# The last routed group takes six tiles instead of four, two tiles stay dense instead of four, and the layer norms of the last batches are moved between the gathers

## The chip, the cores and the metric

One core of one Trainium2 chip runs the whole program. The metric is device time in microseconds (us), median over runs. TensorE (PE) does the matrix products, VectorE (DVE) and ScalarE (ACT) the elementwise work, GpSimd (POOL) some elementwise work and all indirect DMAs (scatters and gathers of rows by an index), SyncE (SP) issues nearly all other DMAs.

## The reference, cut to what matters

The input is x of shape (4, 1024, 256) in float32: B = 4 batches of S = 1024 tokens. Two blocks follow each other, each added to its input and then layer-normalised (mean and variance over the 256 features, eps 1e-5, no scale or shift).

```python
x = layernorm(x + attention(x))   # 16 heads of 16, causal, window of 64 tokens back
x = layernorm(x + moe(x))

def moe(x):                                   # 4096 tokens, 256 features
    scores = sigmoid(x @ router_w.T)          # 16 experts
    sc = scores + e_bias
    # 4 groups of 4 experts; the sum of a group's two best picks 2 groups; then the 4 best experts of these
    tw = scores[chosen] / sum * 2.5           # weights of the 4 chosen experts
    y_e = (silu(x @ gate_e.T) * (x @ up_e.T)) @ down_e.T      # 128 hidden features for each of 16 experts
    return sum_over_chosen(tw * y_e) + shared(x)              # shared: the same form with 2 * 128 hidden features
```

## The kernel before, in words

A tile is 128 tokens, a chunk is 512 tokens (four tiles), a batch is two chunks, so there are eight chunks, 0 to 7. Attention runs as 16 rounds of 13 steps. Two slots belong to each step: slots are numbered h, and the attention ends at slot `tail` = 416. All mixture-of-experts work is cut into jobs, and the function `plan()` puts each job of each engine in a slot; PE takes at most one job in a slot. Every engine then walks through its own slots in order (`fill(h)`), so the plan sets the order of each engine's queue and nothing else: each job waits on semaphores for what it needs, and all behind it on that engine wait too. Slots have no fixed duration.

Every product with weights is done in three fp16 products (high by high, high by low, low by high), over two halves of the 256 features, so each output of the first layer takes six matmuls.

*Routed groups.* `GROUPS` holds four groups: three of a whole batch (eight tiles) and one of chunk 6 alone (four tiles). For a group, `chain` normalises a chunk after attention and computes the router's logits (job `lg`, L767), `route` (L1460) selects experts on DVE in parts, `pos` counts on PE, `place` (L1524) computes on DVE where each token's row goes, and POOL scatters the rows of each tile four times (L1190, one indirect DMA for each tile and choice) into a DRAM buffer `rows`, sorted by expert in units of 128 rows. A group with n tiles has 4n + 16 units, which are taken in pairs. For each pair SP loads the rows transposed (L1027), PE computes gate and up (job `gu`, L844: 24 matmuls 128 wide, whose weight address comes from a register that holds the expert), ACT and DVE apply silu and split the product (L1353, L1637, L1360, L1651), PE computes down (job `y`, L857: 12 matmuls 256 wide), ACT scales it (L1368), SP stores it to the DRAM buffer `outs` (L1033). The shared expert of two tiles is two `gu` jobs of 12 matmuls 256 wide and one `ysh` job (L869). When all pairs of a group are stored, POOL gathers four rows for each token (L1198, four indirect DMAs for each tile, into one of two buffers `yg`), DVE adds them with their weights (`combine`, L1716), and each finished chunk is normalised: moments on DVE (L1723, L1729), the power on POOL (`rstd2`, L1150 to L1156), scaling on ACT (`norm2`, L1324), store by SP (L1054).

*The dense chunk.* Chunk 7 (`DENSE`) is not routed. All 18 experts (two shared, 16 routed) run over its four tiles: job `up` (L798, 12 matmuls 512 wide), then ACT (L1341, L1347) and DVE (L1669 times the weight of the expert for each token, which SP broadcasts from `c_dram`, L1044; L1673; L1658), then job `down` (L814, 12 matmuls 256 wide) into two banks that sum over experts. `finish` (L1675) adds the sum, takes the moments, and `norm_half` and `store_half` end the program.

*What sets the order in the tail.* Behind `tail` the plan has, in this order of slots: chain and routing of chunk 6 (lg at tail+5, pos at tail+12), chain of chunk 7 (lg at tail+20), its expert weights, group 3's scatters (tail+16 to tail+26, at 1.5 to a slot), group 2's pairs until tail+45, group 3's shared and routed jobs (tail+41 to tail+90), with `up` 0 to 5 and `down` 0 to 2 between them, group 2's gathers from tail+51, group 3's gathers from tail+96, and `up` 6 to 17 and `down` 3 to 17 until tail+117.

## Time and profile before

| | us |
|---|---|
| median of 3 runs | 1179.46 |
| lowest, highest | 1176.62, 1181.22 |
| the profiled execution's own time | 1183.34 |
| its span, first to last instruction | 1181.6 |
| PE, DVE, ACT, POOL busy | 1025.7, 826.1, 624.5, 462.2 |

The profile comes from one execution with the hardware profiler on. Busy time leaves out register, branch, semaphore and DMA-issuing instructions. "Idle before, releaser" is the time that an engine sat idle ahead of an instruction, and what ended it; "issue" means that the engine waited for nothing that the profile shows. The end of a matmul is modelled, and matmuls overlap, so the pace of PE is read from start to start. PEclk is the clock granted to TensorE as a share of 2.4 GHz.

### The profile page before, as it was taken

How to read it: one execution, taken by the hardware profiler on the slowest of the kernel's cores; microseconds unless marked ns; L12 is line 12 of the kernel's file. 1: busy time of each engine (PE TensorE's matmuls, PEld its weight loads, DVE VectorE, ACT ScalarE, POOL GpSimd, SP SyncE). 2: the span in 40 equal slices, each digit the busy share in tenths (PEclk: the TensorE clock that was granted, in tenths of full speed). 3: DMA queues.
4: the chain of work that ended last, by engine and by line, in shares of the span. 5: the costliest groups of instructions: out<-in, count | busy, mean ns of one | idle time of the engine just before them, and what ended most of it. 6: DMA issues, size and time to landing. Idle time of an engine off the chain costs nothing.

```text
span 1181.6 us, 24711 instructions
## 1 busy us (share of the span) xinstructions
PE 1025.7 (87%) x8538; PEld 585.9 (50%) x8538; DVE 826.1 (70%) x1828; ACT 624.5 (53%) x1416; POOL 462.2 (39%) x676
## 2 busy tenths in 40 slices
PE   8999999898787999988968889979888864997995
PEld 4554444345332555554634445545544453775653
DVE  8788889778965676787647777687564573445575
ACT  4337777665455666654544656644464742433432
POOL 8752122332165122203627463204626735035351
PEclk9999999999888999998989989998989977998998
DMA  5772557433122454433618554523617554688451
GB/s 191 238 247 66 175 190 231 125 95 77 45 86 76 104 105 103 120 61 68 172 62 156 122 130 119 134 46 78 179 68 148 148 117 134 140 178 190 152 180 49
DMA packets 216678, 150.73 MB, mean 128 GB/s; under 512 B 134624, under 2 KB 192736, under 8 KB 216560
## 3 DMA queue, kind: packets, MB, share of 16 engines
q1 hardware_dynamic: 203184, 116.50, 39.0%
q0 software_dynamic: 10752, 29.37, 7.7%
q10 hardware_dynamic: 2624, 3.28, 0.9%
q8 instruction: 75, 1.23, 0.4%
q14 instruction: 43, 0.35, 0.1%
HBM read 52.46 MB, written 70.29 MB: 104 GB/s over the span
## 4 chain that ended last, share of the span: by engine, by line
PE 55%; DVE 19%; issue 10%; ACT 5%; POOL 4%; DMA 3%; another core or an unknown queue 2%; SPq 1%; DVEq 0%; POOLq 0%; ACTq 0%
PE bank L844 14%; PE bank L662 11%; PE bank L632 9%; PE bank L645 8%; DVE a_mx L1407 6%; PE bank L857 4%; DVE e_R L1716 2%; PE bank L635 2%; ACT a_PT L1259 2%; DMA k_dram<-p_qk 2%; PE bank L748 1%; PE bank L869 1%; PE bank L677 1%; POOL p_qk L1120 1%
## 5 line engine op out<-in xcount | busy, mean ns | idle before, releaser
L1407 DVE TENSOR_REDUCE a_mx<-bank 128x1 f32<-128x512 f32 (+3 forms) x720 | 421.1, 619 | 189.8 <-PE bank L635 95.1
L1259 ACT ACTIVATE a_PT<-bank 128x512 f32<-128x512 f32 (+4 forms) x832 | 373.2, 498 | 182.0 <-PE bank L645 151.2
L645 PE MATMUL bank<-a_QS,a_KS 113*128 113x512 f16 (+4 forms) x832 | 275.6, 339 | 23.2 <-DVE a_mx L1407 17.0
L632 PE MATMUL bank<-a_KS,a_QS 112*128 112x512 f16 (+4 forms) x832 | 264.5, 338 | 30.4 <-ACT a_PT L1259 16.5
L1145 POOL TENSOR_SCALAR_AFFINE_SELECT a_PT<-a_PT 128x256 f32<-128x256 f32 (+1 forms) x288 | 111.2, 393 | 368.6 <-ACT a_PT L1259 366.6
L662 PE MATMUL bank<-a_PT,a_VG 128*17 128x512 f32 (+4 forms) x1664 | 187.1, 518 | 4.2 <-POOL a_PT L1145 2.4
L1198 POOL DMA_INDIRECT a_pool<-outs,e_slot x112 | 111.2, 993 | 118.9 <-DMA outs<-e_ys 50.9
L1190 POOL DMA_INDIRECT rows<-e_XR,e_slot x112 | 111.8, 998 | 108.3 <-DVEq L1559 80.2
L1353 ACT ACTIVATE e_tq<-bank 128x256 f32<-128x256 f32 x116 | 44.5, 384 | 202.3 <-PE bank L844 150.5
L632 PEld LDWEIGHTS bank<-a_KS,a_QS 112*128 112x128 f16 x832 | 80.6, 99 | 134.7 <-ACT a_PT L1259 66.1
L645 PEld LDWEIGHTS bank<-a_QS,a_KS 113*128 113x128 f16 x832 | 81.8, 100 | 102.7 <-DVE a_mx L1407 37.4
L844 PE MATMUL bank<-e_xt,a_W 128*128 128x128 f16 x1416 | 112.5, 229 | 12.2 <-DVE e_hf L1644 9.6
L635 PE MATMUL bank<-a_tri,a_idb 128*128 128x128 f16 (+1 forms) x576 | 111.8, 213 | 2.1 <-issue 2.1
L844 PEld LDWEIGHTS bank<-e_xt,a_W 128*128 x1416 | 95.1, 102 | 34.8 <-issue 23.2
L857 PE MATMUL bank<-a_W,e_hh 128*128 x352 | 67.3, 288 | 7.2 <-DVE e_R L1706 3.4
L635 PEld LDWEIGHTS bank<-a_tri,a_idb 128*128 128x128 f16 x576 | 55.7, 99 | 30.3 <-issue 3.4
L662 PEld LDWEIGHTS bank<-a_PT,a_VG 128*17 128x17 f32 x1664 | 34.4, 117 | 59.3 <-issue 49.5
L1651 DVE TENSOR_TENSOR e_hl<-e_hf,e_hh 128x256 f16<-128x256 f32 x116 | 49.9, 431 | 14.7 <-ACT e_hh L1360 12.3
L1360 ACT CAST e_hh<-e_hf 128x256 f16<-128x256 f32 x116 | 47.3, 408 | 23.1 <-DVE e_hf L1644 14.7
L1716 DVE SCALAR_TENSOR_TENSOR e_R<-a_pool,e_wk,e_R 128x256 f32<-128x256 f32 x112 | 56.7, 507 | 3.5 <-DMA a_pool<-outs,e_slot 0.5
L1368 ACT ACTIVATE e_ys<-bank 128x512 f32<-128x512 f32 x88 | 52.3, 597 | 10.8 <-PE bank L857 4.4
L1637 DVE SCALAR_TENSOR_TENSOR e_hf<-bank,e_tq 128x256 f32<-128x256 f32 x34 | 14.3, 424 | 57.5 <-ACT e_tq L1353 50.0
(184 smaller groups left out, 1371.6 us busy)
## 6 DMA issues: line engine op xcount, KB each, us to landing
outs<-e_ys SPq DMA_DIRECT2D x88, 256.0 KB
rows<-a_pool SPq DMA_DIRECT2D x48, 256.0 KB, 3.6
q_dram<-p_qk SPq DMA_DIRECT2D x16, 256.0 KB, 2.8
k_dram<-p_qk SPq DMA_DIRECT2D x16, 256.0 KB, 3.9
v_dram<-p_vs SPq DMA_DIRECT2D x8, 512.0 KB, 7.2
a_QS<-q_dram SPq DMA_DIRECT2D x64, 64.0 KB
a_KS<-k_dram SPq DMA_DIRECT2D x64, 64.0 KB
a_VG<-v_dram SPq DMA_DIRECT2D x16, 256.0 KB
```

The costliest lines, as they stand in the source:

```text
L632: mm = pe.matmul(ps[:, at:at + hi - lo], QS[p][0:MR, t // NT, h, t % NT * P:t % NT * P + P], KS[p][0:MR, piece, h % 2, 0:hi - lo], start=T ...
L635: mm = pe.matmul(ps[:, at + m0 - lo:at + hi - lo], idb[:], tri[:, m0 - P * t - WIN:m1 - P * t - WIN], start=False, stop=True)
L645: pe.matmul(ps[:, 0:(qc + 1) * CH - q0], KS[p][0:MR + 1, kt // NT, h % 2, kt % NT * P:kt % NT * P + P], QS[p][0:MR + 1, qc, h, q0 - qc * C ...
L662: mm = pe.matmul(otbank[32 * h:32 * h + HD + 1, q0 - qc * CH:CH], VG[p][:, kt, h:VW:HG], PT[(p + i) % 2][:, h, 0:(qc + 1) * CH - q0], star ...
L844: mm = pe.matmul(ps[:, up * 2 * P + at:up * 2 * P + at + v], weights(e, (2 * up + lo) * D + k * P, P), tall[k][part], start=(i == 0), stop ...
L857: mm = pe.matmul(ps[:, v * D:v * D + D], o[q % NHB][:, v * P:v * P + P], weights(e, at, D), start=(i == 0), stop=(i == 2))
L1145: pool.affine_select(out=a, in_=a, compare_op=ALU.is_ge, fill=0.0, base=q0 - (kt * P - WIN), pattern=[[0, 2], [1, w]], channel_multiplier= ...
L1190: pool.indirect_dma_start(rows[b % 2], bass.IndirectOffsetOnAxis(ap=slot[b % 3][:, at, k:k + 1], axis=0), XR[:, at, :], None).then_inc(sca ...
L1198: pool.indirect_dma_start(yg[i % 2][:, k, :], None, outs[b % 2], bass.IndirectOffsetOnAxis(ap=slot[b % 3][:, at, k:k + 1], axis=0)).then_i ...
L1259: act.activation(PT[(G + i) % 2][:, h, 0:w], bank("ST", G, i, h)[:, 0:w], ACT.Exp)\
L1407: dve.tensor_reduce(mx[:, piece, t // NT, heads[0]:heads[0] + n, t % NT], bank("S", G, u)[:, 0:n * w].rearrange("p (h k) -> p h k", h=n), ...
L1716: ins = dve.scalar_tensor_tensor(zz, yg[i % 2][:, k, :], wk[b % 3][:, at, k:k + 1], zz, op0=ALU.mult, op1=ALU.add)
```

## The change

- `GROUPS`: the last group covers tiles 0 to 5 of the last batch (chunk 6 and half of chunk 7): 4 * 6 + 16 = 40 units, 20 pairs, against 32 units and 16 pairs. It needs the routing of both chunks, which is now one list `ROUTES`, and the position job `pos` of group 3 comes behind the second chunk's routing.
- The dense part keeps the last two tiles (`NDT = 2`, 256 tokens). Two experts are computed in one `up` and one `down` job: nine iterations in place of 18; each `up` has 24 matmuls 256 wide, each `down` 12 of 256, into one bank.
- The routed dense iterations (1 to 8) come no earlier than two slots ahead of the last `y` of group 3 (`AHEAD = 2`); iteration 0 (the two shared experts) may come earlier.
- Groups 2 and 3 gather into four buffers in place of two (`sum_of`, `FOUR_FROM`): two new ones lie in the attention's output `O`.
- Group 2's pairs are spread from tail-20 to tail+10 (before: tail-24 to tail).
- The last four `y` of group 3 come four slots behind their `gu` (before: seven); `store_y` comes two slots behind `y` (before: three).
- The norm of group 2's second chunk (5) and of chunk 6 come some slots later, among or behind the gathers of group 3 (`wait`). Before, chunk 6 was normalised at the very end.
- Chunk 7 ends in two halves (`end_of_halves`): tiles 2, 3 (dense) and then tiles 0, 1 (routed), each with its moments, power, shift, scaling (one tile on DVE, one on ACT) and its own store.

```diff
-GROUPS = [(b, 0, BT) for b in range(B - 1)] + [(B - 1, 0, NT)]
+NDT = 2
+DC = NDT * P
+GROUPS = [(b, 0, BT) for b in range(B - 1)] + [(B - 1, 0, BT - NDT)]
+ROUTES = [(b, 0, BT) for b in range(B - 1)] + [(B - 1, half * NT, NT) for half in range(NH2)]
...
+ND = NX // 2
+NSD = NSH // 2
...
+def end_of_halves(at, act, dve, pool, sp):
+
+    dve[at - 1].append(("moments", 1))
+    pool[at].append(("rstd_half", 1))
+    dve[at + 1].append(("shift", 1))
+    act[at + 2].append(("norm_half", 1))
+    sp[at + 3].append(("store_half", 1))
+    dve[at + 2].append(("moments", 0))
+    pool[at + 3].append(("rstd_half", 0))
+    dve[at + 4].append(("shift", 0))
+    act[at + 5].append(("norm_half", 0))
+    sp[at + 6].append(("store_half", 0))
...
-    if n == NX - 1:
-        at = max(h, w)
-        act[at].append(("norm2", DENSE - 1))
-        sp[at + 1].append(("store", DENSE - 1))
-        dve[at + 1].append(("finish",))
-        pool[at + 1].append(("rstd_end",))
-        act[at + 2].append(("norm_half",))
-        for i in range(2):
-            sp[at + 3].append(("store_half", i))
+    if n == ND - 1:
+        end_of_halves(max(h + 2, w), act, dve, pool, sp)
...
+            if late or c % NH2:
+                for n in range(RPARTS):
+                    dve[at + 2 + n].append(("route", g + (late and c % NH2), n))
+        q = put(("pos", g), at + RPARTS + 2)
...
+        if g == B - 2:
+            lo = max(lo, tail + BEGIN)
...
-            last[g] = y = put(("y", g, n), q + (5 if q < tail else 7))
+            last[g] = y = put(("y", g, n), q + (5 if q < tail else 4 if g == B - 1 and n >= NPB[g] - 4 else 7))
             second.append(y)
             act[y + 1].append(("y_out", g, n))
-            sp[y + 3].append(("store_y", g, n))
+            sp[y + 2].append(("store_y", g, n))
...
             if t % NT == NT - 1:
-                c = chunk_of(g, t)
+                wait = 6 if g == B - 2 else 2 if g == B - 1 else 0
                 dve[w + 2].append(("aggr2", c))
-                pool[w + 3].append(("rstd2", c))
-                if c < DENSE - 1:
-                    act[w + 4].append(("norm2", c))
-                    sp[w + 5].append(("store", c))
+                pool[w + 3 + wait].append(("rstd2", c))
+                act[w + 4 + wait].append(("norm2", c))
+                sp[w + 5 + wait].append(("store", c))
...
-    for n in range(NX):
-        h = max(h + 1, ready[DENSE]) if n < NSH else max(h + 1, weighed + 1)
+    for n in range(ND):
+        h = max(h + 1, ready[DENSE]) if n < NSD else max(h + 1, weighed + 1, last[B - 1] - AHEAD)
...
+FOUR_FROM = TILES_TO[2]
+BEGIN = -20
+AHEAD = 2
 RPARTS = 5
-LEFT = 0
+LEFT = 10
...
+    yg = yg + [O[:, i].rearrange("p j d -> p (j d)").rearrange("p (k d) -> p k d", k=TOPK) for i in range(NH2)]
...
+            def dense_experts(n):
+                return range(2 * n + NE, 2 * n + NE + 2) if n < NSD else range(2 * (n - NSD), 2 * (n - NSD) + 2)
...
                     for up, name in enumerate(("gates", "ups")):
                         ps = take(ring, name, n)
-                        i = 0
-                        for lo, xx in ((0, x1h), (0, x1l), (1, x1h)):
-                            for k in range(KD):
-                                mm = pe.matmul(ps[:], weights(e, (2 * up + lo) * D + k * P, P), xx[:, k, at:at + CH],
-                                               start=(i == 0), stop=(i == 5))
-                                i += 1
+                        for v, e in enumerate(dense_experts(n)):
+                            i = 0
+                            for lo, xx in ((0, x1h), (0, x1l), (1, x1h)):
+                                for k in range(KD):
+                                    mm = pe.matmul(ps[:, v * DC:v * DC + DC], weights(e, (2 * up + lo) * D + k * P, P),
+                                                   xx[:, k, S - DC:S], start=(i == 0), stop=(i == 5))
+                                    i += 1
...
-                    for j in range(NT):
-                        y = sums[j // 2][:, j % 2 * D:j % 2 * D + D]
+                    for j in range(NDT):
+                        y = sums[0][:, j * D:j * D + D]
+                        for v, e in enumerate(dense_experts(n)):
...
-                        on.wait_ge(f["comb_done"], i - 1)
-                        pool.indirect_dma_start(yg[i % 2][:, k, :], None, outs[b % 2], bass.IndirectOffsetOnAxis(
-                            ap=slot[b % 3][:, at, k:k + 1], axis=0)).then_inc(gathered[i % 2], 16)
+                        buf, _, past_tile = sum_of(i)
+                        on.wait_ge(f["comb_done"], past_tile + 1)
+                        if i >= FOUR_FROM:
+                            on.wait_ge(f["ont_ready"], NC * KD)
+                        pool.indirect_dma_start(yg[buf][:, k, :], None, outs[b % 2], bass.IndirectOffsetOnAxis(
+                            ap=slot[b % 3][:, at, k:k + 1], axis=0)).then_inc(gathered[buf], 16)
```

## Rows read from the trace of the kernel before

**Rows 1.** From the page: each engine's busy us, share and instructions.
```profile
PE 1025.7 (87%) x8538; PEld 585.9 (50%) x8538; DVE 826.1 (70%) x1828; ACT 624.5 (53%) x1416; POOL 462.2 (39%) x676
```
**Rows 2.** Windows of the tail: length, busy us by engine, clock, DMA.
```profile
980.00:1000.00 20.00, 8.13 (x66) 5.90 (x66) 5.68 (x15) 3.65 (x9) 15.14 (x16) 0.68 0.41 130
...
1100.00:1120.00 20.00, 20.00 (x146) 13.24 (x145) 12.55 (x29) 8.30 (x18) 6.38 (x8) 1.00 0.46 146
```
**Rows 3.** PE's timeline: one dense iteration, up and down, and the next.
```profile
1109.29 2.75 PE L798 MATMUL bank<-e_x1hl,a_W 128*128 128x512 f16 x12
1111.88 1.47 PE L814 MATMUL bank<-a_W,a_QS 128*128 128x256 f16 x12
1113.19 2.75 PE L798 MATMUL bank<-e_x1hl,a_W 128*128 128x512 f16 x12
```
**Rows 4.** The chain of waits (start, us): a y and a gu job.
```profile
1010.51 1.50 PE bank L857 x12
1012.00 1.88 PE bank L844 x24
```
**Rows 5.** PE's timeline: two shared gu jobs, 256 wide, and what follows.
```profile
1037.07 2.78 PE L844 MATMUL bank<-e_x1hl,a_W 128*128 128x256 f16 x24
1039.68 1.53 PE L844 MATMUL bank<-a_PT,a_W 128*128 128x128 f16 x24
```
**Rows 6.** Groups of PE's instructions, 1042 to 1104 us.
```profile
L844 PE MATMUL bank<-a_KS,a_W 128*128 128x128 f16 x216 | 20.2, 231 | 9.0 <-issue 8.9
```
**Rows 7.** Timelines of PE and SP: the last y job and its store.
```profile
1115.78 0.38 PE L857 MATMUL bank<-a_W,e_hh 128*128 x2
...
1123.63 0.36 SPq L1033 DMA_DIRECT2D outs<-e_ys  x1
```
**Rows 8.** POOL's timeline: group 3's first, eighth and last gather.
```profile
1126.90 1.08 POOL L1198 DMA_INDIRECT a_pool<-outs,e_slot  x1 [8.48 <-DMA outs<-e_ys]
...
1136.33 0.94 POOL L1198 DMA_INDIRECT a_pool<-outs,e_slot  x1 [0.30 <-issue]
...
1150.12 1.21 POOL L1198 DMA_INDIRECT a_pool<-outs,e_slot  x1 [0.30 <-issue]
```
**Rows 9.** The chain of waits: a last gather and the combine behind it.
```profile
1106.04 5.97 DMA a_pool<-outs,e_slot
1112.04 0.49 DVE e_R L1716
```
**Rows 10.** Timelines of DVE, POOL, SP: the last combine, the end.
```profile
1154.50 2.04 DVE L1716 SCALAR_TENSOR_TENSOR e_R<-a_pool,e_wk,e_R 128x256 f32<-128x256 f32 x4
...
1170.97 0.75 DVE L1687 BATCH_NORM_STATS2 e_st<-e_R 128x6 f32<-128x256 f32 x2
...
1172.42 1.01 POOL L1171 TENSOR_TENSOR e_rstd<-e_ve,a_mhalf 128x4 f32<-128x4 f32 x1 [9.83 <-DVE e_ve L1692]
...
1173.66 0.74 DVE L1698 TENSOR_SCALAR e_R<-e_R,e_rstd,e_nm 128x256 f32<-128x256 f32 x2
...
1174.78 0.90 SPq L1049 DMA_DIRECT2D out<-e_R  x2
```
**Rows 11.** Groups of instructions, 980 to 1003.5 us, of PE and of POOL.
```profile
L844 PE MATMUL bank<-a_PT,a_W 128*128 128x128 f16 x24 | 4.1, 241 | 13.8 <-issue 13.8
...
L1190 POOL DMA_INDIRECT rows<-e_XR,e_slot x16 | 15.6, 973 | 5.3 <-issue 4.6 <-DVEq L1559 0.7
```
**Rows 12.** The same for 822 to 858 us, inside the attention.
```profile
L632 PE MATMUL bank<-a_KS,a_QS 112*128 112x64 f16 x4 | 0.6, 190 | 2.6 <-issue 2.6
...
L1190 POOL DMA_INDIRECT rows<-e_XR,e_slot x22 | 21.5, 977 | 5.7 <-issue 5.7
```
**Rows 13.** Timelines: logits of chunks 6 and 7, first scatter.
```profile
963.95 0.28 PE L767 MATMUL bank<-a_rwh,e_x1hl 128*128 128x16 f16 x4 [3.73 <-DVE e_x1hl L1625]
...
980.28 1.12 POOL L1190 DMA_INDIRECT rows<-e_XR,e_slot  x1 [0.75 <-DVEq L1559]
...
1003.30 0.27 PE L767 MATMUL bank<-a_rwh,e_x1hl 128*128 128x16 f16 x4 [0.41 <-issue]
```

More of the change, by code:

```diff
@@ L212, in plan @@
             ready[c], at = chain(c, e, 0 if c == NC - 2 else 1)
-        gap = 1
-        for n in range(RPARTS):
-            dve[at + 2 + gap * n].append(("route", g, n))
-        q = put(("pos", g), at + gap * RPARTS + 2)
+            if late or c % NH2:
+                for n in range(RPARTS):
+                    dve[at + 2 + n].append(("route", g + (late and c % NH2), n))
+        q = put(("pos", g), at + RPARTS + 2)
         for n in range(PPARTS):
@@ L222, in plan @@
         routed[g] = q + 4 + steps_of(g, tiles_ * TOPK)
-    sp[tail - 14].append(("load_res", DENSE))
-    pool[tail - 10].append(("add_bo", DENSE))
-    ready[DENSE], at = chain(DENSE, tail + 3, 1)
-    for n in range(RPARTS + 1):
-        dve[at + 2 + n].append(("route", NGR, n))
-    at = put(("cT",), at + RPARTS + 4)
+    dve[q + PPARTS + 1].append(("route", len(ROUTES) - 1, RPARTS))
+    at = put(("cT",), q + PPARTS + 3)
     act[at + 1].append(("cTs",))
@@ L483, in program @@
     res_loaded = [f["res_loaded0"], f["res_loaded1"]]
-    gathered = [f["gathered0"], f["gathered1"]]
+    gathered = [f[f"gathered{i}"] for i in range(4)]
+    yg = yg + [O[:, i].rearrange("p j d -> p (j d)").rearrange("p (k d) -> p k d", k=TOPK) for i in range(NH2)]
     scattered = [f["scattered0"], f["scattered1"]]
@@ L1047, in fill @@
                         at = DENSE * CH + i * 2 * P
-                        on.wait_ge(d[f"out{i}"], 2)
+                        for n in range(2):
+                            on.wait_ge(d[f"out{n}"], 2 - i)
                         sp.dma_start(out[at:at + 2 * P, :].rearrange("(j p) n -> p j n", p=P),
@@ L1168, in fill @@
                         rstd_(0, a[0], f["var_done"], f["eps_done"], f["neg_done"], f["pow_done"], f["rstd_done"])
-                    elif what == "rstd_end":
-                        on.wait_ge(d["eps_done"], 1)
-                        pool.tensor_tensor(rstd[0][:], ve[0][:], mhalf[:], op=ALU.pow).then_inc(d["rstd_done"], 1)
+                    elif what == "rstd_half":
+                        i, = a
+                        half = slice(2 * i, 2 * i + 2)
+                        on.wait_ge(d["eps_done"], 2 - i)
+                        pool.tensor_tensor(rstd[0][:, half], ve[0][:, half], mhalf[:, half], op=ALU.pow)\
+                            .then_inc(d["rstd_done"], 1)
                     elif what == "rstd2":
@@ L1326, in fill @@
                     elif what == "norm_half":
-                        on.wait_ge(d["shift_done"], 1)
-                        for j in range(2):
-                            act.activation(x1_of(DENSE)[:, j, :], x1_of(DENSE)[:, j, :], ACT.Identity, bias=nm[0][:, j:j + 1],
-                                           scale=rstd[0][:, j:j + 1]).then_inc(d["out0"], 1)
+                        i, = a
+                        on.wait_ge(d["shift_done"], 2 - i)
+                        j = 2 * i
+                        act.activation(x1_of(DENSE)[:, j, :], x1_of(DENSE)[:, j, :], ACT.Identity, bias=nm[0][:, j:j + 1],
+                                       scale=rstd[0][:, j:j + 1]).then_inc(d["out0"], 1)
                     elif what == "cTs":
@@ new lines, in fill @@
+                    elif what == "moments":
+                        i, = a
+                        x1, half = x1_of(DENSE), slice(2 * i, 2 * i + 2)
+                        on.wait_ge(f["rstd_done"], NC)
+                        on.wait_ge(f["x1_done"], NC * NT)
+                        if i:
+                            on.wait_ge(d["down_done"], ND)
+                            zz = x1[:, half, :].rearrange("p j n -> p (j n)")
+                            dve.scalar_tensor_tensor(zz, bank("sum")[:], 1.0 / WSC, zz, op0=ALU.mult, op1=ALU.add)\
+                               .then_inc(d["z_done"], 1)
+                            on.wait_ge(d["z_done"], 1)
+                        for j in range(2 * i, 2 * i + 2):
+                            dve.bn_stats(st[0][:, j, :], x1[:, j, :]).then_inc(d["stats_done"], 1)
+                        on.wait_ge(d["stats_done"], 4 - 2 * i)
+                        for j in range(2 * i, 2 * i + 2):
+                            dve.bn_aggr(mv[0][:, j, :], st[0][:, j, :]).then_inc(d["var_done"], 1)
+                        on.wait_ge(d["var_done"], 4 - 2 * i)
+                        dve.tensor_scalar(ve[0][:, half], mv[0][:, half, 1], EPS, None, op0=ALU.add).then_inc(d["eps_done"], 1)
+                    elif what == "shift":
+                        i, = a
+                        x1, half, j = x1_of(DENSE), slice(2 * i, 2 * i + 2), 2 * i + 1
+                        on.wait_ge(d["rstd_done"], 2 - i)
+                        dve.scalar_tensor_tensor(nm[0][:, half], mv[0][:, half, 0], -1.0, rstd[0][:, half], op0=ALU.mult,
+                                                 op1=ALU.mult).then_inc(d["shift_done"], 1)
+                        on.wait_ge(d["shift_done"], 2 - i)
+                        dve.tensor_scalar(x1[:, j, :], x1[:, j, :], rstd[0][:, j:j + 1], nm[0][:, j:j + 1],
+                                          op0=ALU.mult, op1=ALU.add).then_inc(d["out1"], 1)
```

125 lines of the change are left out of this document (56 added, 69 removed).

## The prediction

> **What bounds the kernel now.** I read the page's busy shares first [rows 1]: PE is busy for 87% of the span and no other engine for more than 70%, so PE is the first suspect, but the share mixes the attention, which the change hardly touches, with the tail, which it rebuilds. So I read windows of the tail next [rows 2]. They show two regimes. From 1100 us PE has no gap at all: it is in the dense chunk. From 980 to 1000 us it is busy for 8.13 of 20 us, while POOL is at work for 15.14. Group 3's last `y` begins at 1115.78 [rows 7], and the end follows from two strands that part there. PE's strand: an iteration of the dense chunk takes 1111.88 - 1109.29 = 2.59 for `up` and 1.31 for `down`, 3.90 us together [rows 3], and twelve `up` and fifteen `down` are left: 1115.8 + 1.3 + 12 * 2.59 + 15 * 1.31 = 1167.8, about 1169 with the wait of the last `down` for its operands; moments, power, scaling and store follow, to 1181.6. POOL's strand: 16 gathers from 1126.90 to 1151.3 [rows 8], the last combine at 1154.50 [rows 10]. PE's strand ends last, by more than 10 us. What decides behind the change is thus when the last `y` comes, and which strand is then the longer.
>
> **PE's work.** Removed: 18 dense iterations of 3.90 = 70.2. Put in: nine iterations. A new `up` is 24 matmuls 256 wide; the two shared `gu` jobs are just that, and the next job starts 1039.68 - 1037.07 = 2.61 later [rows 5]. A new `down` is 12 matmuls 256 wide as before, 1.31 [rows 3]. So 9 * 3.92 = 35.3, and the dense chunk gives back 34.9. Added: four pairs. A `y` takes 1012.00 - 1010.51 = 1.5 with its start at the start of the run [rows 4], 1.31 by the 256-wide pace; a `gu` 2.2 (216 matmuls of this kind in 20.2 us are 94 ns each [rows 6]): 4 * 3.5 = 14.0. One more couple of shared jobs with its `ysh`: 2.61 + 1.3 = 3.9. Net 34.9 - 17.9 = 17 us of PE less in all.
>
> **But the last `y` comes no earlier by that.** Ahead of it lay `up` 0 to 5 and `down` 0 to 2, 6 * 2.59 + 3 * 1.31 = 19.5 us; with `AHEAD = 2` only iteration 0's `up` stays, 2.6. So ahead of the last `y`: + 14.0 + 3.9 + 2.6 - 19.5 = + 1.0. The later start of group 2's pairs (tail-20 for tail-24) takes `gu` jobs out of the attention and puts them behind it; the attention ends earlier by the same, at nothing net. With PE's idle time in the tail as before, the last `y` starts at 1115.8 + 1.0 = 1116.8.
>
> A second way to the same number goes by the data. Group 3 now needs the logits of chunk 7. Before they came at 1003.30, behind a stall of PE [rows 11, 13]; without it they would be at about 986. From chunk 6's logits to its first scatter were 980.28 - 963.95 = 16.3 us [rows 13]; six tiles in place of four cost DVE one or two tenths on each of some ten instructions, about 1 us. So the scatters start at 1003; each takes (15.6 + 4.6) / 16 = 1.26 us of POOL [rows 11], 24 of them 30.3, eight more than before or + 10.1. They end at 1033; no load of rows may start before. Four us for the transposed load (my choice: a gather's landing is 5 [rows 9]; 2 to 7 stay possible) give the first routed `gu` at 1037, and PE has until then 36.4 us of other work (1003.30 to 1039.68 [rows 5, 13]) from 986, so the data are late, not PE. Then 20 pairs of 3.5 less one `y`, and 9 us of "issue" as in this stretch before [rows 6]: 1037 + 69 + 9 = 1115. I take 1116.8.
>
> **From the last `y` to the end.** PE's strand: 1.3 + 8 * 3.92 + two last steps of 1.3 = 35 us, 1152 us: no longer the bound. POOL's strand becomes it. Out of PE, through ACT, store and landing took 1126.90 - 1115.78 = 11.1 [rows 7, 8], of which most was ACT's queue: the dense casts stood ahead of the copy out. Now at most one or two such casts do: between 5 and 11, I take 8. Then 24 gathers: eight took 1137.3 - 1126.9 = 10.4 [rows 8], 1.30 each, so 31.2; the ninth and the thirteenth waited for a buffer, about 3 us. With four buffers only tiles 4 and 5 wait, for combines 0 and 1, which are queued on DVE behind the dense products: 0 to 4 us, I take 1. Landing behind the last gather's issue: from 1107.0 to 1112.04, 5 [rows 9]; 2 to 6, I take 4. Combine 2.1 [rows 10], the first half's shift and scaling ahead of the second's moments on DVE 0.6, moments of two tiles 1.2 (0.75 for the statistics, the rest small), power 1.1, shift and one tile each on ACT and DVE 0.9, from the store's issue to the end 6.8 [rows 10]. Sum: 8 + 31.2 + 1 + 4 + 2.1 + 0.6 + 1.2 + 1.1 + 0.9 + 6.8 = 56.9, against 65.8 before. The end is at 1116.8 + 56.9 = 1173.7, 7.9 us less than the span of 1181.6. The profiled execution took 1183.3, 3.9 above the median of 1179.5 and 2.1 above the highest of the three; its excess lies in no row that I change. So 1179.5 - 7.9 = 1171.6 us.
>
> **Costed at nothing.** DVE: 18 us of dense products go, 4 pairs, 8 more combine steps of 0.5 come [rows 10], all ahead of the last combine; it has slack beside PE. If that cover is gone (a dense product waits for its weights, and the combines stand behind it), the gathers of tiles 4 and 5 pay, which is the 0 to 4 above. Chunk 6's norm, which stood in the end, now lies beside the last combines; on POOL it is 2.5 us of small instructions which could fall in front of chunk 7's power: 0 to 2.5, nothing taken, since they wait only for a combine that is two tiles older. The extra four buffers for group 2 shorten its gathers, which had 20 us of slack to group 3's (1107.0 to 1126.9 [rows 8, 9]).
>
> **The stall, and a rule against the trace.** From 980 to 1003.5 PE has one `gu` of 24 matmuls with 13.8 us of "issue" idle in it, no semaphore waited for; POOL runs 16 scatters back to back in just that time [rows 11]. With 22 scatters spread between masks, in the attention, PE's largest such gap is 2.6 us in 36 [rows 12]. In the gathers' stretch, 9.0 us of the same idle stand before `gu` matmuls [rows 6], and none in the window from 1100 us, where the dense chunk runs beside gathers [rows 2]. It looks like code that comes late while indirect DMAs run without a pause. The Trainium skill (Runtime: NRT & Kernel Launch, Instruction fetch mechanics) says that crossing a block of instructions is "one DMA tail-bump, mostly hidden", which the 13.8 us here contradict; by that rule the stall would be chance and might be absent afterwards, which is rival B. The trace speaks rather for rival A.
>
> **Rivals.**
> A, slower: PE stalls for as long as indirect DMAs run back to back beside `gu` jobs. The scatters are then a train of 30 us instead of 20, beside group 2's `gu` jobs (+ 10), and with four buffers group 2's first gathers are a train of 16 instead of 8, now beside group 3's `gu` jobs (+ 8 to 10). The last `y` moves by some 19 and so does the end: 1171.6 + 19 = 1190.6. It decides as soon as more than 8 us of it come true. For it: the long stall lies inside the scatters' train [rows 11]. Against: the 9 us of the gathers' stretch are much less than its gathers' time, and the data are not there before 1037 anyway, so part of the scatters' stall is time that PE has to wait in.
> B, faster: no long stall. PE then waits for the rows alone, and the 9 us of "issue" before `gu` go: last `y` near 1107, end 9 less: 1163.
> C, no change: the POOL strand is longer at each choice: 11 for the way out, 4 for the waits, 6 for the landing, 2.5 for chunk 6's norm: + 10.5 at most, about + 7: 1178.5, within 0.5% of before. That the change does not do what it says would show as this, too: PE's 17 us are saved behind a strand that they do not shorten.
>
> **Numbers.** Forecast 0.47, A 0.22, B 0.15, C 0.16. The time is the likeliest, 1171.6. Its own range is 1165 to 1178; with B's and most of A's the range is 1158 to 1190. A measurement of this kernel can tell about 0.5%, 5.9 us, from no change: faster is below 1173.6, slower above 1185.4. The forecast is faster in three quarters of its own chance (0.35, the rest is the same), B always (0.15), C in a quarter (0.04), and A's mildest cases give 0.02: 0.56. Slower is the most of A: 0.20. Same: 0.24.
>
> **What would show it.** Right: dense windows with `up` groups at 24 matmuls 256 wide in 2.6 us; the last `y` at 1113 to 1121; 24 gathers behind it with gaps of 0.3 us; PE's last matmul 15 us or more ahead of the last combine. Wrong: a run of "issue" idle before L844 that covers the scatters' 30 us (A), or none (B); gathers that wait for combines for over 4 us (C); PE's last `down` later than the last combine, which would say that the strands have not changed places.

## The result and the profile after

The changed kernel took 1195.97 us (median of 4 runs, 1192.17 to 1202.68); the kernel before, on the same chip, 1178.04 (1174.14 to 1181.22): a ratio of 1.0167, interval 1.0138 to 1.0196. It is slower, by 18 us where I forecast 8 us less, and the time lies outside the range of 1158 to 1190. The profiled execution took 1195.27 with a span of 1193.5.

Page of the kernel after, as [rows 1]:

```profile
span 1193.5 us, 24895 instructions
...
PE 1000.6 (84%) x8586; PEld 586.6 (49%) x8586; DVE 819.8 (69%) x1822; ACT 620.4 (52%) x1415; POOL 477.2 (40%) x694
```

PE's work did become less: 1025.7 us busy before, 1000.6 after. The span grew all the same, so what grew is PE's idle time. Windows of the tail after, as [rows 2] (length, busy us and instructions of PE, PEld, DVE, ACT, POOL, then clock, DMA share, GB/s):

```profile
980.00:1000.00 20.00, 13.38 (x131) 11.29 (x128) 11.15 (x31) 5.23 (x12) 11.24 (x12) 0.77 0.42 135
1000.00:1020.00 20.00, 3.68 (x19) 1.86 (x19) 0.46 (x2) 1.65 (x4) 12.15 (x13) 0.50 0.44 130
1046.00:1066.00 20.00, 8.02 (x77) 5.03 (x74) 1.88 (x5) 1.06 (x3) 15.17 (x16) 0.66 0.54 123
1100.00:1120.00 20.00, 17.20 (x177) 13.75 (x175) 13.41 (x36) 10.25 (x24) 5.82 (x8) 0.91 0.71 197
```

In the second PE is busy for 3.68 of 20 us, DVE for 0.46 and ACT for 1.65, while POOL issues scatters. In the third PE has 8.02 and POOL issues 16 gathers. Groups of instructions after, from the first scatter to the end of the long stall, as [rows 11]:

```profile
L1218 POOL DMA_INDIRECT rows<-e_XR,e_slot x24 | 23.4, 974 | 24.5 <-DVEq L1596 17.5 <-issue 7.0
L868 PE MATMUL bank<-a_KS,a_W 128*128 128x128 f16 x37 | 6.4, 296 | 19.3 <-issue 19.3
```

L868 is the `gu` job, L1218 the scatter. Where before had 13.8 us of idle with no semaphore waited for, there are now 19.3. PE's waits after, 940 us to the end (us in all, times, longest):

```profile
PE bank L868 <- issue: 41.1, 40, 2.6
...
PE bank L824 <- issue: 5.0, 6, 1.3
PE bank L812 <- issue: 3.7, 1, 3.7
```

All of PE's lines with "issue" come to 51.6 us there; the same stretch of before has 25.4. (L812, the transposes of the combine weights, is a wait of another kind: on chips without a stall the same 3.6 us are put down to DVE's queue. Without it 47.9 us are left.) Timelines after of the last `y` with what stands around it (L824 is `up`, L838 `down`), and of POOL's gathers of group 3, as [rows 7, 8]:

```profile
1121.86 2.13 PE L868 MATMUL bank<-a_PT,a_W 128*128 128x128 f16 x24
1123.83 5.40 PE L824 MATMUL bank<-e_x1hl,a_W 128*128 128x256 f16 x48
1129.07 0.38 PE L881 MATMUL bank<-a_W,e_hh 128*128 x2
...
1129.72 1.47 PE L838 MATMUL bank<-a_W,a_QS 128*128 128x256 f16 x12
1131.03 2.78 PE L824 MATMUL bank<-e_x1hl,a_W 128*128 128x256 f16 x24
```

```profile
1135.22 1.08 POOL L1229 DMA_INDIRECT a_pool<-outs,e_slot  x1 [7.46 <-DMA outs<-e_ys]
...
1154.78 0.94 POOL L1229 DMA_INDIRECT a_O<-outs,e_slot  x1 [0.30 <-issue]
1162.55 1.43 POOL L1229 DMA_INDIRECT a_pool<-outs,e_slot  x1 [6.83 <-DVEq L1760]
...
1168.88 1.40 POOL L1229 DMA_INDIRECT a_pool<-outs,e_slot  x1 [0.94 <-DVEq L1760]
...
1173.08 0.95 POOL L1229 DMA_INDIRECT a_pool<-outs,e_slot  x1 [0.30 <-issue]
```

The last `y` starts at 1129.07, 13.3 us later than before; from there to the end are 64.4 us, where before had 65.8 and I had forecast 56.9. The first 16 gathers run unbroken; those of tile 4 wait 6.83 us for combine 0.

### The profile page after: what moved, and what is told of

Same layout as the page of the kernel before. It is cut to its first block, busy times and chain, and to the rows that moved or that the text cites. A ratio compares the mean times of both kernels' runs of the same rounds, so it can differ in the third digit from the quotient of the medians.

```text
span 1193.5 us, 24895 instructions
## 1 busy us (share of the span) xinstructions
PE 1000.6 (84%) x8586; PEld 586.6 (49%) x8586; DVE 819.8 (69%) x1822; ACT 620.4 (52%) x1415; POOL 477.2 (40%) x694
## 3 DMA queue, kind: packets, MB, share of 16 engines
q8 instruction: 75, 1.23, 0.4%
## 4 chain that ended last, share of the span: by engine, by line
PE 55%; DVE 19%; issue 10%; POOL 6%; ACT 4%; another core or an unknown queue 2%; DMA 2%; SPq 1%; ACTq 0%; DVEq 0%; POOLq 0%
PE bank L868 14%; PE bank L685 10%; PE bank L655 9%; PE bank L668 8%; DVE a_mx L1439 6%; PE bank L881 4%; PE bank L824 2%; DVE e_R L1756 2%; PE bank L658 2%; ACT a_PT L1290 2%; PE bank L893 1%; POOL a_pool L1229 1%; POOL rows L1218 1%; POOL a_PT L1170 1%
## 5 line engine op out<-in xcount | busy, mean ns | idle before, releaser
L655 PE MATMUL bank<-a_KS,a_QS 112*128 112x512 f16 (+4 forms) x832 | 263.6, 337 | 24.9 <-ACT a_PT L1290 9.9
L685 PE MATMUL bank<-a_PT,a_VG 128*17 128x512 f32 (+4 forms) x1664 | 184.4, 511 | 9.2 <-POOL a_PT L1170 8.6
L1218 POOL DMA_INDIRECT rows<-e_XR,e_slot x120 | 119.2, 993 | 128.4 <-DVEq L1596 97.8
L1229 POOL DMA_INDIRECT a_pool<-outs,e_slot x96 | 94.6, 986 | 93.9 <-issue 54.7
L868 PE MATMUL bank<-e_xt,a_W 128*128 128x128 f16 x1368 | 106.1, 229 | 5.2 <-issue 2.4
L868 PEld LDWEIGHTS bank<-e_xt,a_W 128*128 x1368 | 91.2, 102 | 24.1 <-issue 13.6
L881 PE MATMUL bank<-a_W,e_hh 128*128 x368 | 70.4, 288 | 11.0 <-DVE e_R L1745 3.4
L1674 DVE SCALAR_TENSOR_TENSOR e_hf<-bank,e_tq 128x256 f32<-128x256 f32 x43 | 18.0, 422 | 82.1 <-ACT e_tq L1385 75.6
L868 PE MATMUL bank<-a_KS,a_W 128*128 128x128 f16 x504 | 44.8, 243 | 29.0 <-issue 28.9
L1688 DVE TENSOR_TENSOR e_hl<-e_hf,e_hh 128x256 f16<-128x256 f32 x122 | 54.3, 446 | 20.6 <-ACT e_hh L1392 18.3
L1400 ACT ACTIVATE e_ys<-bank 128x512 f32<-128x512 f32 x92 | 54.5, 599 | 24.9 <-remote 13.8
L1392 ACT CAST e_hh<-e_hf 128x256 f16<-128x256 f32 x122 | 49.8, 408 | 29.6 <-DVE e_hf L1681 14.7
```

Source lines behind the costliest of these rows:

```text
L655: mm = pe.matmul(ps[:, at:at + hi - lo], QS[p][0:MR, t // NT, h, t % NT * P:t % NT * P + P], KS[p][0:MR, piece, h % 2, 0:hi - lo], start=T ...
L685: mm = pe.matmul(otbank[32 * h:32 * h + HD + 1, q0 - qc * CH:CH], VG[p][:, kt, h:VW:HG], PT[(p + i) % 2][:, h, 0:(qc + 1) * CH - q0], star ...
L868: mm = pe.matmul(ps[:, up * 2 * P + at:up * 2 * P + at + v], weights(e, (2 * up + lo) * D + k * P, P), tall[k][part], start=(i == 0), stop ...
L881: mm = pe.matmul(ps[:, v * D:v * D + D], o[q % NHB][:, v * P:v * P + P], weights(e, at, D), start=(i == 0), stop=(i == 2))
L1218: pool.indirect_dma_start(rows[b % 2], bass.IndirectOffsetOnAxis(ap=slot[b % 3][:, at, k:k + 1], axis=0), XR[:, at, :], None).then_inc(sca ...
L1229: pool.indirect_dma_start(yg[buf][:, k, :], None, outs[b % 2], bass.IndirectOffsetOnAxis(ap=slot[b % 3][:, at, k:k + 1], axis=0)).then_inc ...
```

## Experiments

Five sets on five chips; each ratio is against the kernel before on the same chip. "Issue idle" is PE's idle time put down to no semaphore. A "train" is a run of indirect DMAs that POOL issues one behind the other, and the "stall" is PE's issue idle beside one.

**The scatter train, in the kernel before (chip 14, before 1178.16).** e1 issues each of group 3's scatters twice:

```
+    if b == 3:
+        pool.indirect_dma_start(rows[2], <the same offsets and rows>).then_inc(scattered[b % 2], 16)
     pool.indirect_dma_start(rows[b % 2], ...
```

> The kernel before, but each of group 3's 16 scatters is issued twice, the copy into a buffer that nobody reads: 32 indirect DMAs back to back, 40 us instead of 20, everything else in its order. Theory A (PE's instructions come late while indirect DMAs run back to back; the stall lasts from some 5 us after the train's start to 3 us after its end): the issue idle before the gu matmuls grows from 13.8 to about 33 us, and the whole kernel by 15 to 20 us. Rival N (the stall belongs to that place in the code or to chance, and the train is beside it by accident): the stall stays near 14 us, the scattered rows come 20 us later but group 3's first routed gu began 36 us behind the stall, so the time stays within 5 us.

1209.39 us, 1.0264 (1.0239 to 1.0289): 31 us more. e2 leaves them out:

```
+    if b == 3:
+        rest()      # a power of 128x4 on POOL, which waits for the one before it
+        continue
     pool.indirect_dma_start(rows[b % 2], ...
```

> The kernel before with group 3's 16 scatters left out: in the place of each one POOL computes a power of 128x4 (about 1.05 us), so POOL is busy as long but issues no DMA; group 3's rows stay what the buffer holds. Theory A: no long issue stall of PE between 975 and 1005 us, the logits of chunk 7 come about 15 us earlier, the kernel is 10 to 16 us faster. Rival P (what hurts is POOL being busy, or PE's code alone): the stall of 14 us stays, time within 3 us.

1166.34 us, 0.9899 (0.9879 to 0.9919): 12 us less. Windows of e1 over the train, then of e2 over the place where it was, and e1's waits from 975 to 1025:

```profile
980.00:1020.00 40.00, 8.17 (x59) 4.86 (x59) 4.10 (x13) 2.07 (x5) 29.69 (x31) 0.59 0.29 112
```

```profile
975.00:1005.00 30.00, 27.71 (x319) 23.67 (x320) 18.01 (x65) 14.26 (x36) 16.30 (x16) 0.89 0.60 137
```

```profile
PE bank L844 <- issue: 24.6, 19, 2.6
PE bank L767 <- issue: 11.1, 8, 2.6
```

POOL works as long in e2 in the scatters' place, and PE has 27.71 of 30 us. So it is the transfers, not POOL's work, and the loss grows with the train: 0.7 us of issue idle for none, 13.8 for 16, 35.7 (the two lines above) for 32. Rivals N and P fall. Theory A's numbers hold in e2; in e1 its idle time does (about 33 us), its time does not (15 to 20 us more, not 31), and the other 11 us are not explained.

**Shorter gather trains and pauses, in the changed kernel (same chip).** e3 gives it back its two gather buffers, so that group 2's first train has 8 gathers:

```
-    FOUR_FROM = TILES_TO[2]
+    FOUR_FROM = 99
```

> The changed kernel with two gather buffers as before: group 2's gathers are a train of 8 and then fours, group 3's too. Theory A: the issue idle at group 2's first gathers falls from some 16 us to 2 to 6, the one beside the dense part (13 us) goes, the scatters' stall of 22 us stays; 8 to 14 us faster than the changed kernel (1196), at 1182 to 1188. Rival G (four buffers help as they are meant to; the loss lies in the later scatters alone): slower than the changed kernel by 0 to 8 us.

1196.82 us, 1.0151 (1.0127 to 1.0175). I had expected 8 to 14 us of the loss back by theory A, and none came: the time is the change's. PE's issue idle from 940 us on did fall, from 51.6 to 44.1 us: 20.3 beside the scatters (19.3 in the change), 18.8 beside group 2's gathers (22.1), 1.3 in the dense part (6.5). A train of 16 gathers cut in two saves little, because other trains follow it. Why even these 7.5 us do not show in the time is open; in one profile each, group 3's first scatter came 8 us later in e3 (993.7 after 985.4), and on other chips the changed kernel itself has it 3 and 6 us later (988.0 in e10, 991.5 in e17). e4 puts the power (1.07 us) behind each scatter of group 3 and each gather of groups 2 and 3:

```
     pool.indirect_dma_start(...)
+    if b == 3: rest()        # at the gathers: if b >= 2
```

> The changed kernel with a pause behind each scatter of group 3 and each gather of groups 2 and 3: POOL computes a power of 128x4, about 1.05 us, so that the indirect DMAs follow each other every 2.4 us in place of 1.26. Theory A in the form that PE's code gets through in the pauses: the issue idle in the tail falls from 40 to under 10 us; against it stands POOL's own time, 24 * 1.1 = 26 us later rows and 26 us longer last gathers, so the sum is between 10 us faster and 15 us slower than the changed kernel. If only the sum of outstanding DMAs mattered and not their closeness, the stall would stretch with the train to some 45 us at the scatters.

1226.50 us, 1.0392 (1.0351 to 1.0433). PE's waits of e4 from 990 us to the end:

```profile
PE bank L870 <- DMA a_KS<-rows: 29.5, 1, 29.5
PE bank L883 <- DVE e_hl L1702: 20.3, 4, 13.8
...
PE bank L870 <- issue: 1.8, 4, 0.8
```

The issue idle is gone (1.8 us), with all 56 transfers still there. What takes its place is PE's wait for rows and hidden values behind trains twice as long. So it is transfers without a pause, not transfers, that stop PE. The time is 30 us above the change's all the same; I had 15 as the most.

**The same on a chip that has no stall (chip 1, before 1103.82).** e5 is the changed kernel with group 3's scatters left out as in e2; e6 has e4's pauses with a subtract (0.21 us) in place of the power; e7 has the power behind every fourth transfer only; e8 is the kernel before with e6's pauses.

```
e6, e8  -  pool.tensor_tensor(nap, ..., op=ALU.pow)
        +  pool.tensor_tensor(nap, ..., op=ALU.subtract)
e7      +  if b == 3 and k == 3: rest()     # at the gathers: if b >= 2 and k == 3
```

> The changed kernel with group 3's 24 scatters left out (in their place 24 powers of 128x4 on POOL, so group 3's rows are stale; the rest is computed). It sizes the scatters' share of the loss. Theory A (PE stalls beside indirect DMAs issued back to back; 21.8 us in the scatters' train, some 25 in the gathers' trains): the stall at 990-1020 us is gone, that of the first gathers of group 2 (16.3 us) stays, and the time is 1196 - 22 = 1174 us, 1170 to 1180. Rival G (the loss over the kernel before lies in the gathers alone, since before has a stall of 13.8 us at its scatters too, worth 12 us there): 1196 - 12 = 1184. Rival D (the rows of group 3 are late anyway, and PE only waits another way): above 1190.

> The changed kernel with a subtract of 128x4 on POOL, which waits for the one before it, behind each scatter of group 3 and each gather of groups 2 and 3 (estimate 0.2 to 0.4 us; with a power of 1.05 us there the stalls were gone, but the trains took 54 us and the time was 1226). Theory A1 (any break on POOL between two indirect DMAs lets PE on): stalls under 5 us in all, trains of 24 in 36 to 40 us; 1196 - 35 of stall + 12 of longer trains = 1165 to 1178. Rival A2 (only the share of time that POOL issues indirect DMAs counts): stall still 0.7 of 40 us and trains longer, 1190 to 1200.

> The changed kernel with the power of 1.05 us behind each fourth indirect DMA only (scatters of group 3, gathers of groups 2 and 3). Theory A3 (a train must have lasted some 5 us before PE stalls, and a break ends it): trains of four last 5 us, so stalls under 8 us in all; the trains are 6 us longer; 1196 - 32 + 8 = 1168 to 1176. Rival (one break of 1 us lets PE take a few instructions and no more): stall as before, time 1196 to 1204.

> The kernel before with the short subtract behind each scatter of group 3 and each gather of groups 2 and 3. Theory A1: the stall of 13.8 us at the scatters and some 9 us at the gathers go, trains are 4 us longer; with the scatters left out this kernel took 1166; here 1164 to 1172. Rival A2: 1178 to 1184.

1099.76 us (0.9965, 0.9942 to 0.9989); 1114.72 (1.0109, 1.0072 to 1.0146); 1115.86 (1.0118, 1.0081 to 1.0155); 1105.70 (1.0018, 0.9995 to 1.0040). None of my numbers fits, for a reason that none of my theories held: the kernel before takes 1104 us here and 1178 there. In e5 group 2's first 16 gathers are still unbroken (28 follow each other, from 987.0 to 1021.7), and this is e5's window over them, to be set beside the third window of the kernel after:

```profile
987.00:1007.00 20.00, 18.93 (x202) 14.32 (x199) 10.01 (x24) 8.37 (x20) 15.41 (x16) 1.00 1.13 238
```

PE is busy for 18.93 of 20 us in place of 8.02, at the same pace of POOL. This chip does not stall; the four runs say nothing on pauses, except that they lengthen the trains.

**Where does the chip come in? (chip 0, before 1181.96).** e9 and e10 are the two kernels unchanged, e11 and e12 are e6 and e8 again.

> The kernel before, unchanged, for its profile on the chip of the next three. On the chip of the last four runs every kernel was about 6% faster than on the first, and their profiles had 2.5 to 3.3 us of issue idle on PE in all, where the profile shown of before has 42.2 and that of the change 69.2. Theory S (the stall is a property of the chip, or of its state): about 1178 us with over 30 us of issue idle on PE, or about 1104 us with under 5, and nothing between. Rival (the short pauses cured it there): about 1104 with over 20 us of issue idle in this kernel.

> The changed kernel, unchanged. With theory S: where e9 has its 30 us or more, this one is 1.5 to 2% slower than before and PE loses over 20 us in the scatters' train; where e9 has under 5, it is within 0.5% of before, 1099 to 1109 us: the last y 9 to 13 us later than before's (measured with the scatters left out: 9), the way from it to the end 14 us shorter (measured: 52.4 after 66.7). Rival (the 24 scatters cost PE beside their stall as well): 1110 or more on such a chip.

> The changed kernel with the short subtract behind each scatter of group 3 and each gather of groups 2 and 3, a second time. Where e10 stalls: theory A1 (any break lets PE on) gives 1165 to 1180, rival A2 (the share of time counts) 1190 to 1200. Where e10 does not stall: 1.1% over before as the first time, 1110 to 1120; the pauses only lengthen the trains.

> The kernel before with the same short pauses, a second time. Where e9 stalls: A1 gives 1160 to 1170 (the 13.8 us at the scatters and most of 9 us at the gathers go), A2 1176 to 1184. Where e9 does not: within 0.5% of before, as the first time.

1183.51 us (0.9996, 0.9964 to 1.0028), 1201.69 (1.0188, 1.0111 to 1.0265), 1195.92 (1.0103, 1.0033 to 1.0173), 1180.93 (0.9988, 0.9950 to 1.0026). A chip of the first kind, as theory S has it: issue idle of 43.7 us in e9. The change's 20 us are there again: the last `y` starts 20.4 us later in e10 than in e9 (1131.9 after 1111.5), and the way from it to the end is 65.8 us, not 67.6. The short pauses (train of 24 in 32.4 us, not 29.4) took the scatters' stall, L812's wait left out, from 20.6 to 15.5 us: a fifth of a microsecond is no cure. Theory A1 falls; both times lie in A2's ranges.

**Sizing the change without the stall, and the fourth-transfer pause (chip 7, before 1103.38).** e13 is e5 again, e15 is e7 again, e16 the kernel before with e7's pauses. e14 has the changed kernel's `up` with half the instructions for the same columns:

```
-    for lo, xx in ((0, x1h), (0, x1l), (1, x1h)):
-        for k in range(KD):
-            mm = pe.matmul(ps[:, v * DC:v * DC + DC], <weights k>, xx[:, k, S - DC:S], ...)
+    for i, (lo, xx) in enumerate(((0, x1h), (0, x1l), (1, x1h))):
+        mm = pe.matmul(ps[:], <weights v>, xx[:, v, <512 columns>], ...)
```

> The changed kernel with group 3's scatters left out (POOL powers in their place; group 3's rows are stale), a second time, for a chip where PE stalls. There: the scatters' stall of 22 us goes, the gathers' 23 us and the dense pieces' 7 us stay. Theory A: 1.019 - 22/1180 = 1.000 of before, 0.995 to 1.006. Rival G (the change loses by its gathers, the scatters cost before 12 us too): 1.009 and more. On a chip without the stall 0.9965 again.

> The changed kernel with each dense up as 12 matmuls of 512 columns in place of 24 of 256: the same columns and PE time, half the instructions (the dense result is another: every second product is left out and its neighbour computed twice as wide). Theory H (PE starves for instructions, so pieces with half as many per us do not stall): where it stalls, the 7 to 8 us of issue idle in the dense part go, combine 0 comes sooner, the gathers of tiles 4 and 5 wait 1 to 3 us in place of 7.8, and the time is 4 to 8 us under the change's, 1.012 to 1.016 of before. Rival (the dense stall has to do with the weights or operands, not the number of instructions): as the change, 1.019. Without the stall: as the change there.

> The changed kernel with the power of 1.05 us behind each fourth transfer of group 3's scatters and of groups 2 and 3's gathers, a second time, for a chip where PE stalls. Theory A3 (the stall needs some 5 us of unbroken train to start, and a break of 1 us ends it): under 10 us of stall in the trains, 0.995 to 1.005 of before. Rival A2 (only the share of time that transfers are issued counts, as the short pauses suggest: 19.3 us of stall in 32.4 against 22.5 in 29.4): 19 to 21 us of stall at the scatters, 1.010 to 1.020.

> The kernel before with the same pause behind each fourth transfer. A3: the stall of 14 to 16 us at its 16 scatters falls under 5 us: 0.990 to 0.994 (with the scatters left out it was 0.990). A2: 0.997 to 1.002. Without the stall: 1.000 to 1.003.

1096.80 us (0.9940, 0.9925 to 0.9955), 1109.05 (1.0049, 1.0027 to 1.0070), 1120.60 (1.0133, 1.0077 to 1.0189), 1105.24 (1.0020, 1.0003 to 1.0036). Again a chip without the stall: issue idle of 2.0 to 3.1 us per program. To leave out the scatters is worth something here, too: e13 takes 12 us less than e14, which has them (and the other dense pieces), and no stall is in either. The pause behind every fourth transfer was thus never tried where it could help; that stays open. e14 stands here for the change without the stall, and its last `y` starts at 1050.9, e16's at 1033.2: 17.7 us later, and 55.4 us to the end in place of 67.4. PE's waits of e14 from 930 us on:

```profile
PE bank L865 <- DMA a_KS<-rows: 4.8, 1, 4.8
PE bank L812 <- DVEq L1538: 3.6, 1, 3.6
PE bank L865 <- issue: 2.6, 5, 1.0
```

**The scatters' share, and the number of instructions (chip 15, before 1182.31).** e17 is the changed kernel again, e18 is it with e5's and e14's edits together.

> The changed kernel, unchanged, a third time. On a chip without the stall: 1.003 to 1.007 of before (the kernel with wide dense pieces had 1.005: last y 12 to 18 us later, of it 5.4 for two more ups ahead of it than I counted and 5 for the rows of group 3; the way from it to the end 12 us shorter). On a chip with it: 1.017 to 1.020, as twice before. Rival (narrow dense pieces cost time by themselves): 1.010 and more without the stall.

> The changed kernel with group 3's scatters left out and each dense up as 12 matmuls of 512 columns (group 3's rows stale, the dense result another one). On a chip with the stall, theory A and H: no stall where the scatters were; under 2 us of issue idle in the dense pieces that run beside 24 gathers; the gathers' stalls beside gu jobs (16 + 5 us) as they were; the time 22 + 5 us under the change's, 0.994 to 1.000 of before. Rival G: 1.008 or more. Rival to H: 7 us of issue idle in the dense pieces. On a chip without it: 0.994 to 0.997, as with the scatters alone left out.

1203.52 us (1.0169, 1.0117 to 1.0221) and 1180.52 (0.9966, 0.9936 to 0.9997). A chip with the stall. e18 is 23 us faster than e17: 0.7 us of issue idle is left where the scatters were (19.0 in e17), and 14.6 beside the 16 gathers as before (15.1). The ratio lies in A's range and G falls. But the 23 us are not the price of the scatters' stall alone: on chip 7 the scatters were worth up to 12 us with no stall. H falls too. Timeline of e18's PE in the dense part, beside gathers that run unbroken from 1125.4 on:

```profile
1136.47 2.75 PE L826 MATMUL bank<-e_x1hl,a_W 128*128 128x512 f16 x12
1139.06 1.15 PE L839 MATMUL bank<-a_W,a_QS 128*128 128x256 f16 x8
1141.31 0.27 PE L839 MATMUL bank<-a_W,a_QS 128*128 128x256 f16 x1 [1.10 <-issue]
...
1146.28 0.58 PE L826 MATMUL bank<-e_x1hl,a_W 128*128 128x512 f16 x1 [1.07 <-issue]
1148.37 1.31 PE L826 MATMUL bank<-e_x1hl,a_W 128*128 128x512 f16 x2 [1.50 <-issue]
...
1154.03 2.72 PE L826 MATMUL bank<-e_x1hl,a_W 128*128 128x512 f16 x6 [0.81 <-issue]
```

The wide pieces stall as well: 8.7 us of issue idle before L826 and L839, against 7.0 in e17's narrow ones. They are as wide as those of the kernel before, which had 0.5 us of issue idle beside group 3's gathers. What differs is the train: there a gather waited for a combine after the first eight; here 20 follow each other, and PE stops some 15 us in. Half as many instructions in the dense pieces did not help.

## Why the prediction was wrong

**The failed step: "With PE's idle time in the tail as before, the last `y` starts at 1115.8 + 1.0 = 1116.8."** It started at 1129.07, and the idle time was not as before. I had the row that shows the stall [rows 11] and the contrast [rows 12], named the mechanism as rival A with + 18 to 20 us, and gave it 0.22. Measured: one train of 24 scatters in place of 16 cost PE 19.3 us and not 13.8; group 2's gathers in one train of 16 cost 14.4 us where 8 had cost 1.7. From 940 us on PE has 22 us more of issue idle (47.9 against 25.4), on chip 0 26 us more (50.4 against 24.2), L812's wait left out. A's own numbers, + 10 and + 8 to 10, had the sum right and the split wrong: + 5.5 at the scatters and + 12.7 at these gathers.

**The stall is only about half of the miss.** With the stall the change is 18 to 21 us slower (three times), without it about 5 us (e14), and I had forecast 8 us faster. So some 13 us of the miss are there with no stall at all, and 13 to 16 come with it. This is an estimate, since e14 has other dense pieces. The profiles, one of each kernel, say where. Without the stall the last `y` comes 17.7 us later (e14 against e16, which is before with pauses) and the way from it to the end is 12.0 us shorter. With the stall it comes 13.3 us later (20.4 on chip 0), and the way is only 1.4 (1.8) us shorter. So the same step would have failed without the stall, by terms that I mis-sized (below, under `AHEAD`), and what the stall adds shows for the most part behind the last `y`. And the two first spans differ by 11.9 us, the medians by 17.9: I had taken 3.9 us off because before's profiled execution was slow, and the change's was not (1195.27, median 1195.97).

**Why I set A so low.** I argued that "the data are not there before 1037 anyway", so that PE would only stall in time in which it had to wait. But in the stall group 2's `gu` jobs stood still, which wait for no such data, and everything behind them moved. No wait for group 3's rows shows in the trace after. I also assumed that the attention's end would stay where it was, with chunk 7's logits at 986. With group 2's pairs moved behind it, the attention's last score product came at 930.5 and not at 946.6, the logits at 968.9, and group 3's first scatter at 985.4 and not at 1003.

**"With `AHEAD = 2` only iteration 0's `up` stays, 2.6."** Mis-read: three `up`s stand ahead of the last `y`, two of them just before it (1123.83 to 1129.07). That is 5.2 us more in the term, so + 6.2 and not + 1.0 with no stall at all. The rest of the 17.7 us of e14 over e16 are its waits: 4.8 for the rows (the load needed 6.4 us behind the last scatter, from 975.6 to 982.0, where I took 4), 3.6 for the combine weights, which job `cT` transposes (a wait that before does not have, and that I did not see), and some 3 that are not named: PE's busy time up to there is 950.8 in e14 and 940.8 in e16, 10.0 more, where the two terms give 6.2.

**From the last `y` to the end, 56.9.** With no stall the sum was right: 55.4 in e14, 24 gathers from 1059.3 to 1089.4 with no gap. With the stall it was 64.4. The way out was 6.15, the gathers 31.0 and 7.8 of waits (I took 1), and 19.5 from the last gather to the end, where I had 16.7. The waits are the point that I missed: beside 16 gathers in a row the static dense pieces stall too (6.5 us) and DVE's work behind them comes late, so that combine 0, whose last gather was issued at 1139.6, frees the buffer only at 1162. That is rival C's condition ("gathers that wait for combines for over 4 us"), with A as its cause. I had priced each alone.

**Right.** The dense windows have 24 matmuls 256 wide in 2.6 us. PE's busy time fell, by 25 us in the two first profiles, where the lower clock swells both numbers; without the stall from 997.8 (e8) to 976.1 to 978.6 (e5 to e7) on one chip and from 993.2 (e16) to 978.2 to 981.8 (e13 to e15) on the other, 11 to 22 us where I counted 17. The strands changed places (PE's last matmul ends at 1171.0, the last combine starts at 1179.3), though by 8 us and not by 15. A transfer takes 1.25 us of POOL. The change does what it says. Where there is no stall it is 0.5% slower all the same (e14, with other dense pieces; the change itself was never run on such a chip).

**The rule, and late code.** By the Trainium skill (Runtime: NRT & Kernel Launch, Instruction fetch mechanics) a crossing of blocks is "one DMA tail-bump, mostly hidden". I wrote that the 13.8 us contradict it. They do not: the trace records the loads of instruction blocks, and the stall lies between them (in before, between the loads at 984.4 and 1005.9 us, with PE at its pace again from 1003.3 on). The page of the kernel after has 75 of them, 1.23 MB, on queue 8, and 43, 0.34 MB, on queue 14. DMA queues after, from 985.4 to 1019.4 us (the scatters' train and its stall), and from 1019.4 to 1046 (packets, MB, share):

```profile
q0 software_dynamic: 1152, 3.15, 26.4%
q1 hardware_dynamic: 3504, 1.85, 19.5%
```

```profile
q1 hardware_dynamic: 8166, 3.20, 52.0%
q8 instruction: 3, 0.05, 0.8%
q14 instruction: 1, 0.01, 0.1%
```

Neither queue 8 nor 14 loads anything in the stall, while PE still issues a matmul every one to three microseconds; the last load before it starts at 983.6, the next at 1021.1, when PE has been back at its pace since 1019.4. From 1050.2 to 1068.9, in the stall beside the gathers, neither loads anything either. If PE had waited for a block, a load should end the wait. So "code that comes late", as I put it, is not borne out in the form of late blocks, and the rule has no part in the miss.

**What stays open.** That unbroken trains of indirect DMAs stop PE is shown (e1, e2, e4). By what way is not. PE's idle time in a train is put down to no semaphore. DVE and ACT do next to nothing either, but the profile puts most of their idle time down to others: in the scatters' train DVE's 24.9 us to ACT, ACT's 18.4 to a releaser that it cannot tell. So it is not shown that they stall by themselves. Why chips differ is open, too.

## What to carry to other kernels

Before you lengthen a run of indirect DMAs, or give it more buffers so that it never pauses, look in the trace for idle time with no semaphore on the engines beside it; if there is any, price the longer run at that share of its length, and do not set it off against waits that it does not touch. Then ask which part of it reaches the end: here 22 us more of idle time were worth 13 to 16. Look for a second chip as well; without it the mis-sized terms, which are half of the miss, would have been put down to the stall. When a rival rests on a row and the forecast on "as before", the row should carry the chance. And price rivals together where one causes the other.

## What the runs showed of the hardware

On chips 14, 0 and 15 PE stops some 5 to 15 us into a train of indirect DMAs issued every 1.25 to 1.4 us, issues a matmul or a few in each 0.7 to 2.8 us until the train's end, and goes on 1 to 4 us later; with one transfer in 2.4 us (e4) it does not stop. On chips 1 and 7 it never does. The kernel before takes 1178 to 1182 us on the one kind and 1103 to 1104 on the other. Windows of the kernel before, and of e16 (which is the same up to 900 us), from the start to the first indirect DMA, a stretch of trains, and a stretch with few transfers (1 in before, 8 in e16):

```profile
0.00:310.00 310.00, 287.51 (x2136) 141.57 (x2137) 257.00 (x503) 190.97 (x407) 116.92 (x182) 0.99 0.49 156
...
530.00:620.00 90.00, 74.67 (x641) 43.47 (x638) 55.84 (x120) 42.26 (x100) 35.70 (x49) 0.91 0.40 98
...
700.00:790.00 90.00, 80.83 (x773) 48.80 (x770) 69.93 (x181) 56.53 (x137) 22.08 (x43) 0.98 0.42 100
```

```profile
0.00:310.00 310.00, 286.79 (x2132) 141.40 (x2133) 256.48 (x502) 190.67 (x406) 116.70 (x183) 0.98 0.49 156
...
530.00:620.00 90.00, 84.02 (x775) 48.85 (x777) 65.49 (x138) 51.46 (x128) 54.15 (x76) 0.98 0.62 143
...
700.00:790.00 90.00, 78.93 (x736) 47.85 (x735) 71.62 (x183) 49.43 (x119) 21.05 (x37) 0.98 0.37 83
```

Up to the first transfer the chips cannot be told apart, and hardly in the stretch with few; in the stretch of trains PE has 74.67 us on the one and 84.02 on the other. The granted clock follows the idle time (0.91 beside 0.98; 0.50 in the middle of the long stall). After the stall of the kernel after it is still 0.50, 1.2 GHz, from 1019.4 to 1023 us, and 1.00 from 1026 on, so PE loses some more.
